# Weights laid out by the host, row-tiled matmuls and a new order of work in a fused attention and mixture-of-experts kernel

## The chip, the cores and the metric

One core of a Trainium2 chip runs the whole kernel. The metric is the device time of one execution in microseconds, from the first instruction to the last. Engines are named as in the profile: PE (matrix engine, its weight loads are PEld), DVE (vector), ACT (scalar), POOL (GpSimd), SP (sync, issues DMAs).

## The reference

`x` is 32 sequences of 32 tokens with 512 features, all fp32. Cut to what matters:

```python
w = weights[subjects]                               # one 32x32 matrix per sequence
c = einsum('bct,bcd->bdt', x, w)                    # mixes the 32 tokens of a sequence
q, k, v = (heads(c @ W.T) for W in (wq, wk, wv))    # 32 heads of 16
q, k = rope(q), rope(k)
p = softmax(where(causal, q @ k.T / 4, -inf))
x = x + (p @ v) @ wo.T
logits = x @ Wr.T + 5 * one_hot(language)           # 8 experts, two best
gates = two best, softmax, scattered to 8
y = x @ W.T + 2 * sum_e gates_e * (x @ A_e.T) @ B_e.T
t = y[:, perm].reshape(-1, 16, 32)                  # 16 blocks of 32 features
t = gelu(einsum('bhd,hdm->bhm', t, up))             # 32 -> 128 per block
t = einsum('bhm,hmd->bhd', t, down)                 # 128 -> 32 per block
x = x + t.reshape(-1, 512)[:, argsort(perm)]
```

## The kernel before

1024 tokens are 8 tiles of 128 (four sequences each); two tiles are a group, and there are four groups (`G` = 4, called groups 0 to 3). Every engine has a list of work written out by hand; semaphores tie the lists. A dense product in fp32 accuracy is `mm3` (lines 433 to 437): operands are split into a high fp32r part (a copy by ACT) and a low one (a subtraction by DVE), and three fp32r matmuls are added. The others are plain fp32 matmuls, each of which the profile shows as two records.

**The beginning.** SP loads wq and x, then waits until POOL's gathered rows of the condition weights (`wg`, line 359) are there, and then loads wk, wv, wo, and in pieces A, B, the router, the permutation, up and down (lines 308 to 332). PE transposes wq, wk, wv, wo, w2, the unpermute matrix, A and the router into PSUM (`prep_w`, line 450; lines 665, 688), ACT copies the high parts, DVE subtracts the low ones. B is permuted by a matmul (`prep_b`, line 655). `up` is laid out as `upP`, 128 x 128 blocks that hold 32 rows of weights and 96 of zeros.

**A group.** `cond` mixes tokens (L460), `qk` and `v` project (L435 to L437 into `ps_A`), DVE and POOL apply the rope (L1030, L1031, L377, L381), both build `kbd`, a block-diagonal copy of k with 8 heads beside each other in 256 columns (L390 on POOL, L1041 on DVE, 128x1024 each). `scores` (L495, L503) adds a causal mask and multiplies, 4 sequences in 4 column strips of 32. DVE subtracts maxima, ACT takes exponentials, DVE sums, POOL normalises (L399), DVE transposes blocks (L1071), ACT copies them into `pbd` by sequence (32x256 each, 8 in `probs_block` for two chunks), and `pv` (L518) multiplies. Then `wo_proj`, `add_x`, `turn_x1` (transposes of x, L539).

**Experts and FFN of a group** run beside the attention of the next: `lora_down`, gates (a chain of some twenty small DVE steps with one exponential on ACT), `experts_base`, `experts_lora`, a split of the result into `y2`, then `ffn_up` (each of 8 calls a bank of 512 columns: two blocks, three fp32r matmuls of 256 columns each, L435 to L437 into `ps_D`), gelu on ACT (L873), `ffn_down` (L614, four column strips), `unpermute` (L628), `add_ffn`. In group 3 the FFN of group 2 runs beside the attention; the FFN of group 3 is the tail, with nothing beside it. PSUM is four rings of two banks (A, S, C, D); each result waits for its bank to be read.

## Time and profile before

| | |
|---|---|
| median of 3 runs | 292.97 us (292.37 to 293.67) |
| the profiled execution | 292.91 us, of which the span of its instructions is 291.1 us |
| PE busy | 257.2 us, 88% of the span, 2293 records |
| PE weight loads | 207.6 us, 71% |
| DVE / ACT / POOL busy | 173.6 / 139.2 / 107.7 us |
| granted PE clock, mean | 0.988 |
| moved by DMA | 11.42 MB, 39 GB/s over the span |

The group whose PE work starts with `cond` of the next group and ends with `wo_proj` repeats: group 1 takes from 91.04 to 150.89 us. A busy PE is one with a matmul in flight, so a record's duration holds its latency; what a matmul costs in a stream is read from the distance of the starts.

### The profile page before, as it was taken

What the parts mean: (1) busy time and instruction counts of PE and PEld (TensorE: products, weight loads), DVE (VectorE), ACT (ScalarE), POOL (GpSimd) and SP (SyncE); (2) the same over time, 40 slices, a digit from 0 to 9 for tenths busy, and PEclk for the clock granted to TensorE, in tenths of its full rate; (3) what the DMA queues carried; (4) which work ended last, traced back from release to release, by engine and by line L of the source; (5) the groups of instructions that cost most, each with busy time, mean ns of one, the idle gap of its engine ahead of it and who ended that gap; (6) DMA issues with size and microseconds to landing.
All of it is one profiled execution on the core that took longest, in us unless ns stands there. A gap on an engine that the chain in (4) does not pass through costs nothing.

```text
span 291.1 us, 5710 instructions
## 1 busy us (share of the span) xinstructions
PE 257.2 (88%) x2293; PEld 207.6 (71%) x2304; DVE 173.6 (60%) x356; ACT 139.2 (48%) x276; POOL 107.7 (37%) x82
## 2 busy tenths in 40 slices
PE   0799398999999999999999999999989964789895
PEld 0689396778766788779776977797759743458764
DVE  0556379998598868464169583741677814335402
ACT  1342364237672336975322359953113597921460
POOL 2636379649840502157806011668060111100000
PEclk9999879999999999999999999999999999999999
DMA  4599603000000000012000000010000000001001
GB/s 127 148 345 254 145 12 134 0 2 1 2 0 2 5 0 2 0 62 84 2 0 2 0 2 2 2 74 0 0 2 2 0 2 0 3 0 73 0 2 72
DMA packets 13498, 11.42 MB, mean 39 GB/s; under 512 B 7576, under 2 KB 9368, under 8 KB 13472
## 3 DMA queue, kind: packets, MB, share of 16 engines
q1 hardware_dynamic: 12608, 9.85, 11.2%
q0 software_dynamic: 576, 1.18, 1.5%
q8 instruction: 18, 0.29, 0.5%
q14 instruction: 8, 0.07, 0.1%
q10 hardware_dynamic: 288, 0.03, 0.1%
HBM read 8.96 MB, written 2.10 MB: 38 GB/s over the span
## 4 chain that ended last, share of the span: by engine, by line
PE 67%; ACT 9%; DVE 9%; DMA 5%; issue 4%; SPq 4%; POOL 1%; ACTq 0%; DVEq 0%
PE ps_D L435 7%; ACT pbd L809 6%; PE ps_A L435 6%; PE ps_S L503 6%; PE ps_A L436 5%; PE ps_A L437 5%; PE ps_D L437 5%; PE ps_D L436 5%; PE ps_C L518 5%; PE ps_D L628 4%; PE ps_C L435 4%; PE ps_C L437 4%; PE ps_C L436 4%; SPq L325 3%; DMA pbd<-in_L_ffn_perm 2%
## 5 line engine op out<-in xcount | busy, mean ns | idle before, releaser
L809 ACT ACTIVATE pbd<-pr 32x256 f32<-32x256 f32 x128 | 53.0, 414 | 14.2 <-PE ps_C L518 7.3
L390 POOL TENSOR_TENSOR kbd<-kr,cst 128x1024 f32<-128x1024 f32 x16 | 35.2, 2221 | 29.1 <-PE ps_S L503 29.1
L399 POOL TENSOR_TENSOR pr<-pr,small 128x512 f32<-128x512 f32 x16 | 16.5, 1049 | 59.8 <-DVE small L1065 59.8
L377 POOL TENSOR_TENSOR rot<-rot,cst 128x512 f32<-128x512 f32 x16 | 20.7, 1292 | 32.4 <-DVE rot L1030 32.3
L873 ACT ACTIVATE act<-ps_D 128x512 f32<-128x512 f32 x32 | 19.0, 598 | 13.1 <-PE ps_D L437 11.5
L518 PE MATMUL ps_C<-pbd,vz 128*32 128x128 f32 x512 | 20.0, 278 | 5.4 <-ACT pbd L809 5.2
L1041 DVE TENSOR_TENSOR kbd<-kr,cst 128x1024 f32<-128x1024 f32 x16 | 24.6, 1555 | 0.0
L435 PE MATMUL ps_A<-xc,wkT 128*128 128x256 f32 x64 | 19.5, 305 | 4.6 <-DVE qr L1031 4.6
L518 PEld LDWEIGHTS ps_C<-pbd,vz 128*32 128x32 f32 x512 | 12.3, 109 | 13.3 <-ACT pbd L809 7.8
L435 PE MATMUL ps_D<-y,upP 128*128 128x256 f32 x64 | 19.6, 305 | 0.8 <-DVE y L997 0.8
L997 DVE TENSOR_TENSOR y<-ps_S,y 128x512 fp32r<-128x512 f32 x8 | 5.4, 677 | 24.7 <-ACT y L809 24.7
L503 PE MATMUL ps_S<-kbd,qr 128*32 128x256 f32 x256 | 17.1, 385 | 2.0 <-issue 1.4
L436 PE MATMUL ps_A<-xc,wkT 128*128 128x256 f32 x64 | 18.8, 294 | 0.0
L437 PE MATMUL ps_A<-xc,wkT 128*128 128x256 f32 x64 | 18.7, 293 | 0.0
L435 PE MATMUL ps_D<-x,w2T 128*128 128x256 f32 x64 | 18.7, 292 | 0.0
L435 PE MATMUL ps_A<-xc,wqT 128*128 128x256 f32 x64 | 18.6, 291 | 0.0
L628 PE MATMUL ps_D<-unperm,y 128*128 128x512 f32 x64 | 17.3, 409 | 0.8 <-DVE y L997 0.8
L436 PE MATMUL ps_A<-xc,wqT 128*128 128x256 f32 x64 | 17.9, 280 | 0.0
L436 PE MATMUL ps_D<-y,upP 128*128 128x256 f32 x64 | 17.9, 279 | 0.0
L436 PE MATMUL ps_D<-x,w2T 128*128 128x256 f32 x64 | 17.9, 279 | 0.0
L437 PE MATMUL ps_D<-x,w2T 128*128 128x256 f32 x64 | 17.9, 279 | 0.0
L437 PE MATMUL ps_D<-y,upP 128*128 128x256 f32 x64 | 17.9, 279 | 0.0
(186 smaller groups left out, 698.5 us busy)
## 6 DMA issues: line engine op xcount, KB each, us to landing
xs<-in_x SPq DMA_DIRECT2D x4, 512.0 KB, 3.9
out<-xs SPq DMA_DIRECT2D x3, 512.0 KB, 2.8
pbd<-in_L_attn_wq SPq DMA_DIRECT2D x2, 512.0 KB, 6.2
act<-in_L_attn_wk SPq DMA_DIRECT2D x1, 1024.0 KB
pr<-in_L_attn_wv SPq DMA_DIRECT2D x1, 1024.0 KB, 9.0
xs<-in_L_attn_wo SPq DMA_DIRECT2D x1, 1024.0 KB
out<-xs SPq DMA_DIRECT2D x2, 256.0 KB, 2.0
pbd<-in_L_cond_A SPq DMA_DIRECT2D x1, 256.0 KB
```

What stands on the lines that cost most here:

```text
L377: pool.tensor_tensor(rv, rv, con("sin").unsqueeze(1).to_broadcast([P, 2 * N // T, T]), ALU.mult).then_inc(rot_sin, 1)
L390: pool.tensor_tensor(kbd[:, c, :, :].rearrange("p b (h s) -> p b h s", h=HC), kv.unsqueeze(2).to_broadcast([P, BT, HC, T]), con("head").un ...
L399: pool.tensor_tensor(pr[:, i, :, :], pr[:, i, :, :], mx[:, i, :].unsqueeze(2).to_broadcast([P, NH // 2, T]), ALU.mult).then_inc(normed, 1)
L435: pe.matmul(dst, hi_l, hi_r, start=start, stop=False, skip_group_check=skip)
L436: pe.matmul(dst, hi_l, lo_r, start=False, stop=False, skip_group_check=skip)
L437: return pe.matmul(dst, lo_l, hi_r, start=False, stop=stop, skip_group_check=skip)
L503: last = pe.matmul(bank(it)[T * b:T * b + T, N * (c % 2):N * (c % 2) + N], qr[:, c, at:at + T], kbd[:, c, b, :], start=False, stop=True, s ...
L518: last = pe.matmul(bank(it)[32 * j:32 * j + 32, P * c:P * c + P], vz[:, t, 4 * c + j, HD * e:HD * e + 2 * HD], pbd[:, c % 2, 2 * j + e, :, :],
L628: last = pe.matmul(bank(it)[:, :], y2[:, part, c, P * t:P * t + P], unperm[:, c, :], start=(c == 0 and part == 0), stop=(c == KC - 1 and p ...
L809: return sc.activation(dst, src, ACT.Copy)
L873: sc.activation(act[:, i % 4, :, :], bank(it)[:, :].rearrange("p (h n) -> p h n", h=2), ACT.Gelu).then_inc(s_free(it), 1)
L1041: ve.tensor_tensor(kbd[:, c, :, :].rearrange("p b (h s) -> p b h s", h=HC), kv.unsqueeze(2).to_broadcast([P, BT, HC, T]), con("head").unsq ...
```

## The change

The host hands over all weights transposed or laid out as they are used, and adds a table of column numbers. The program changes with it:

- SP issues every load at once, without a wait; ACT's queue issues two small ones (the ids, the permutation). ACT and DVE split the weights from SBUF in pieces of 128x1024 (`w_his`, `w_los`). PE transposes only w2 (whose rows POOL gathers by the permutation) and B (gathered the same way, `perm_rows`). The unpermute matrix is four comparisons on DVE.
- q's and k's heads are laid out so that a chunk of 128 features is two halves of 64 rows, four heads each. `kbd` holds 128 columns for each sequence, 128x512 for a tile and chunk, and has room for both tiles of a group. `scores` works on a whole tile: two masks, then 32 matmuls of 64 rows, 32 columns and 128 moving columns; the two row halves write to two banks.
- `ffn_up` uses the plain 32x128 blocks of `up` in fp32 on 32 rows each, four row groups into four banks; `y2`'s split into two parts is one copy (`x2_out`), and the doubled weights `upP` are gone.
- `probs_block` copies 32x512 at once in place of 32x256, so 16 copies for a group in place of 32.
- PSUM is three rings: A and S of two banks, F of four in place of C and D.
- The lists of all engines are written in another order.

```diff
-            sp.wait_ge(d_wg[0], 16 * GT)
-            load_w("wk", raw_k)
...
+            load_w("wk")
+            load_w("wv")
+            load_w("wo")
+            sp.dma_start(col_no, cols).then_inc(d_cols, 16)
+            sp.dma_start(raw_a, wa.rearrange("(c p) k -> p c k", p=P)).then_inc(d_w["a"], 16)
...
+            pool.wait_ge(idx_ready, 1)
+            cond_rows(0)
+            pool.wait_ge(d_permc, 16)
+            perm_rows(raw["w2"], w2, d_w["w2"])
+            cond_rows(1)
...
+            for t in range(GT):
+                k_blocks(0, t, 1)
+                k_blocks(0, t, 3)
+            wait_w(pool, "wq")
+            pool.memset(pbd[:, 0, :, :, :], 0.0).then_inc(pbd_zero, 1)
+            perm_rows(raw_b, wb, d_w["b"])
+            cond_rows(2)
+            cond_rows(3)
...
+                        for r in range(2):
+                            rows = slice(P // 2 * r, P // 2 * r + P // 2)
+                            last = pe.matmul(bank(its[r])[T * b:T * b + T, P * c:P * c + P],
+                                             qr[rows, c, at:at + T], kbd[rows, t, c, b, :], start=False, stop=True,
...
-            def ffn_up(g, i):
...
-                    last = mm3(bank(it)[:, N * h:N * h + N], upP[:, 0, c, j, :], upP[:, 1, c, j, :],
-                               y2[:, 0, c, :], y2[:, 1, c, :], True, True)
+            def ffn_up(g, r):
+
+                wait_read(pe, Fi(g, "W", r))
+                for c in (2 * r, 2 * r + 1):
+                    for j in range(4):
+                        it = Fi(g, "UP", r, j)
+                        if c % 2 == 0:
+                            wait_free(pe, it)
+                        at = slice(FD * j, FD * j + FD)
+                        last = pe.matmul(bank(it)[:, N * (c % 2):N * (c % 2) + N], upw[at, c, :], x2[at, c, :],
+                                         start=True, stop=True)
...
                 for b in range(BT):
                     at = slice(T * b, T * b + T)
-                    last = copy(pbd[at, c % 2, :, b, :], pT(2 * t + c // 2)[at, HC * (c % 2):HC * (c % 2) + HC, :])
+                    last = copy(pbd[at, i, :, b, :], pT(2 * t + i)[at, :, :])
...
+            w_los("wq", raw["wq"], WT["wq"], 2)
             blocks(0)
-            prep_los("wq", KC, lambda k, s: WT["wq"][:, s, k, :])
             cond_lo(0, 0)
             cond_lo(0, 1)
...
+                    qk(g + 1, "wk", K_, 0)
+                    ffn_up(g - 1, 0)
+                    qk(g + 1, "wk", K_, 1)
+                    ffn_up(g - 1, 1)
+                    ffn_down(g - 1, 0)
+                    ffn_down(g - 1, 1)
+                    v(g + 1, 0)
+                    for c in range(KC):
+                        pv(g, 0, c)
```

Three places show how instructions move. **PE in group 1, the FFN of group 0**, before (two up calls, the first down call, the next up call; `upP` is the padded weight, `act` the gelu's output):

```order
L435 MATMUL ps_D1<-y2,upP 128x256
L436 MATMUL ps_D1<-y2,upP 128x256
L437 MATMUL ps_D1<-y2,upP 128x256
L614 MATMUL ps_S0<-act,dn 32x256 x4
L435 MATMUL ps_D0<-y2,upP 128x256
L436 MATMUL ps_D0<-y2,upP 128x256
L437 MATMUL ps_D0<-y2,upP 128x256
```

PE at the same work after (`upw` is the plain weight; `wkT` and `wvT` belong to the projections of group 2):

```order
L439 MATMUL ps_A<-xc,wkT 128x256
L440 MATMUL ps_A<-xc,wkT 128x256
L441 MATMUL ps_A<-xc,wkT 128x256
L622 MATMUL ps_F<-x,upw 128x256 x8
L634 MATMUL ps_S<-act,dn 32x256 x8
L439 MATMUL ps_A<-wvT,xc 128x512
L440 MATMUL ps_A<-wvT,xc 128x512
L441 MATMUL ps_A<-wvT,xc 128x512
```

48 up matmuls of a group are 16, in two visits that stand between the projections, and the four down visits are two.

**PE at the start of group 1, the scores**, before (`mask_b` is the mask, `rT` the router of the experts' part):

```order
L460 MATMUL ps_A0<-wbd,xs 128x128 x4
L539 MATMUL ps_C1<-cst,xs 128x128 x4
L495 MATMUL ps_S0<-mask_b,ident_b 128x512
L503 MATMUL ps_S0<-kbd,qr 32x256 x8
L495 MATMUL ps_S1<-mask_b,ident_b 128x512
L503 MATMUL ps_S1<-kbd,qr 32x256 x8
L435 MATMUL ps_C0<-x1,rT 8x256
```

and after:

```order
L469 MATMUL ps_A<-wbd,xs 128x128 x8
L556 MATMUL ps_F<-cst,xs 128x128 x4
L507 MATMUL ps_S<-mask_b,ident_b 128x512 x2
L517 MATMUL ps_S<-kbd,qr 32x128 x32
L439 MATMUL ps_F<-x,rT 8x256
```

16 score matmuls of a tile are 32 of half the width, and both masks stand ahead of them.

**POOL ahead of the first `norm` of group 0**, before (`rot`, `kr`: rope; `pbd`: the zeroing of the buffer for probabilities):

```order
L377 TENSOR_TENSOR rot<-rot,cst 128x512
L381 TENSOR_TENSOR kr<-kr,rot 128x512
L390 TENSOR_TENSOR kbd<-kr,cst 128x1024 x2
L410 MEMSET pbd 128x2048
L390 TENSOR_TENSOR kbd<-kr,cst 128x1024 x2
L399 TENSOR_TENSOR pr<-pr,small 128x512
```

and after:

```order
L379 TENSOR_TENSOR x<-x,cst 128x512
L383 TENSOR_TENSOR kr<-kr,x 128x512
L392 TENSOR_TENSOR kbd<-kr,cst 128x512 x4
L416 MEMSET pbd 128x2048
L369 DMA x<-in_L_cond_B,permc 128x128 x4
L362 DMA wg<-in_L_cond_weights,idx 128x32 x4
L401 TENSOR_TENSOR pr<-pr,small 128x512 x2
```

Eight gather issues now stand between the k blocks and the first normalisation.

## Rows read from the trace of the kernel before

**Rows 1.** Busy time by stretch: length, each engine's busy us, PEclk, DMA share, GB/s.
```profile
0.00:19.20 19.20, 9.04 (x47) 8.44 (x48) 7.14 (x22) 5.01 (x8) 9.30 (x13) 1.00 0.62 183
19.20:43.50 24.30, 19.74 (x155) 19.50 (x154) 15.09 (x33) 11.05 (x22) 12.37 (x11) 0.86 0.65 162
43.50:58.60 15.10, 14.19 (x99) 10.49 (x99) 15.03 (x15) 5.25 (x12) 11.71 (x7) 1.00 0.18 68
58.60:91.04 32.44, 31.23 (x311) 24.80 (x312) 26.93 (x46) 18.96 (x42) 19.58 (x15) 1.00 0.01 2
91.04:150.89 59.85, 59.08 (x548) 47.59 (x550) 36.20 (x78) 30.56 (x61) 22.94 (x16) 1.00 0.05 19
210.80:254.60 43.80, 34.68 (x375) 25.72 (x378) 24.47 (x54) 26.83 (x55) 8.92 (x6) 1.00 0.01 2
254.60:291.10 36.50, 30.13 (x224) 23.79 (x224) 13.13 (x36) 10.93 (x19) 0.00 (x0) 1.00 0.08 29
```

**Rows 2.** Timeline of PE at the FFN of group 0: start, duration, line, shapes.
```profile
109.16 0.39 PE L435 MATMUL ps_D<-y,upP 128*128 128x256 f32 x1
110.83 0.38 PE L435 MATMUL ps_D<-y,upP 128*128 128x256 f32 x1
...
114.60 0.64 PE L614 MATMUL ps_S<-act,dn 128*32 128x256 f32 x8
115.17 0.39 PE L435 MATMUL ps_D<-y,upP 128*128 128x256 f32 x1
```

**Rows 3.** Timeline of PE at the first scores of group 1.
```profile
92.69 1.07 PE L503 MATMUL ps_S<-kbd,qr 128*32 128x256 f32 x16
93.69 0.39 PE L495 MATMUL ps_S<-mask_b,ident_b 128*128 128x512 bf16 x1
94.02 1.07 PE L503 MATMUL ps_S<-kbd,qr 128*32 128x256 f32 x16
```

**Rows 4.** Timeline: the last two `pv` calls of group 1 in one visit.
```profile
140.79 1.08 PE L518 MATMUL ps_C<-pbd,vz 128*32 128x128 f32 x32
```

**Rows 5.** ACT by form: line, tiles, shapes, count | busy us, mean ns.
```profile
L809 ACT ACTIVATE pbd<-pr 32x256 f32<-32x256 f32 x128 | 53.0, 414 | 14.2 <-PE ps_C L518 7.3 <-DVE pr L1071 5.0
L834 ACT ACTIVATE pr<-pr 128x512 f32<-128x512 f32 x16 | 9.3, 623 | 2.3 <-DVE pr L1057 2.2
```

**Rows 6.** Timeline of DVE: k blocks beside POOL's own, and alone.
```profile
46.76 4.63 DVE L1041 TENSOR_TENSOR kbd<-kr,cst 128x1024 f32<-128x1024 f32 x2
...
53.23 1.22 DVE L1041 TENSOR_TENSOR kbd<-kr,cst 128x1024 f32<-128x1024 f32 x1
```

**Rows 7.** POOL by form.
```profile
L390 POOL TENSOR_TENSOR kbd<-kr,cst 128x1024 f32<-128x1024 f32 x16 | 35.2, 2221 | 29.1 <-PE ps_S L503 29.1
...
L377 POOL TENSOR_TENSOR rot<-rot,cst 128x512 f32<-128x512 f32 x16 | 20.7, 1292 | 32.4 <-DVE rot L1030 32.3
...
L359 POOL DMA_INDIRECT wg<-in_L_cond_weights,idx x8 | 7.7, 965 | 8.3 <-DVE idx L1167 6.2 <-issue 2.1
```

**Rows 8.** The beginning: DVE's wait for the gathered rows, and a stretch of full loading.
```profile
12.24 0.74 DVE L1016 TENSOR_SCALAR wbd<-wg,cst 128x64 f32<-128x64 f32 x4 [2.81 <-DMA wg<-in_L_cond_weights,idx]
...
20.00:22.00 2.00, 2.00 (x19) 2.00 (x18) 1.94 (x4) 1.38 (x3) 0.00 (x0) 1.00 1.06 369
```

**Rows 9.** PE after its longest idle time (timeline, and the stretch with its clock).
```profile
35.96 0.58 PE L435 MATMUL ps_A<-xc,wkT 128*128 128x256 f32 x1 [4.56 <-DVE qr L1031]
...
36.00:40.50 4.50, 4.50 (x21) 4.50 (x22) 2.34 (x5) 3.00 (x6) 3.39 (x4) 0.50 0.00 0
```

**Rows 10.** Waits from 210 us on: who waited for whom, us, times, longest.
```profile
PE ps_C L518 <- ACT pbd L809: 5.0, 6, 1.7
```

**Rows 11.** The chain that ended last, its tail.
```profile
283.89 3.95 PE ps_D L628 x16
287.86 0.69 DVE xs L1156
```

More of the change, by code:

```diff
@@ new lines, in _ @@
+            load_w("wk")
[3 more added lines that the diff above has]
+            sp.dma_start(raw_a, wa.rearrange("(c p) k -> p c k", p=P)).then_inc(d_w["a"], 16)
+            with nc.allow_non_contiguous_dma(reason="the router's eight columns, once"):
+                sp.dma_start(raw_r, wr.rearrange("(c p) k -> p c k", p=P)).then_inc(d_w["r"], 16)
+            sp.dma_start(upw[:, :, :], up).then_inc(d_up, 16)
+            sp.dma_start(dn[:, :, :], down).then_inc(d_dn, 16)
@@ L711, in _ @@
                 if g:
-                    for c in range(KC - 1):
+                    for c in range(1, KC):
                         experts_base(g - 1, c)
-                    if g + 1 < G:
-                        cond(g + 1, 1)
+                if more:
+                    qk(g + 1, "wq", Q, 0)
+                if g:
                     turn_gates(g - 1)
-                    experts_base(g - 1, KC - 1)
+                if more:
+                    qk(g + 1, "wq", Q, 1)
+                if g:
@@ new lines, in _ @@
+                    wait_w(pe, "wo")
+                elif more:
+                    qk(g + 1, "wk", K_, 0)
[5 more added lines that the diff above has]
+                    v(g + 1, 0)
+                    for c in range(KC):
+                        pv(g, 0, c)
+                    ffn_down(g - 1, 2)
+                    ffn_down(g - 1, 3)
+                    v(g + 1, 1)
+                    for c in range(KC):
+                        pv(g, 1, c)
+                    unpermute(g - 1, 0)
+                    unpermute(g - 1, 1)
+                else:
+                    ffn_up(g - 1, 0)
+                    pv(g, 0, 0)
+                    pv(g, 0, 1)
+                    ffn_up(g - 1, 1)
+                    ffn_down(g - 1, 0)
+                    ffn_down(g - 1, 1)
+                    pv(g, 0, 2)
+                    pv(g, 0, 3)
+                    ffn_down(g - 1, 2)
+                    ffn_down(g - 1, 3)
@@ L801, in _ @@
+            ffn_up(G - 1, 1)
+            for c in range(KC):
+                ffn_down(G - 1, c)
             for half in range(2):
@@ L910, in _, with gelu @@
[L910 to L912 removed]
+            def gelu(g, r):
+                for j in range(4):
+                    it = Fi(g, "UP", r, j)
+                    wait_full(sc, it)
+                    if g and j == 0:
+                        wait_full(sc, S_down(g - 1, r))
+                    sc.activation(act[:, r, j, :, :], bank(it)[:, :].rearrange("p (h n) -> p h n", h=2), ACT.Gelu
+                                  ).then_inc(s_free(it), 1)
@@ new lines, in _ @@
+            rope(0, 0)
+            w_los("wv", raw["wv"], WT["wv"], 2)
+            rope(0, 1)
+            w_los("wo", raw["wo"], WT["wo"], 2)
+            rope(0, 2)
+            ve.wait_ge(d_cols, 16)
+            for c in range(KC):
+                ve.tensor_scalar(unperm[:, c, :], col_no, permf[:, c:c + 1], None, ALU.is_equal
+                                 ).then_inc(unperm_ready, 1)
+            w_los("a", raw_a, aT, 1)
+            w_los("r", raw_r, rT, 1)
+            rope(0, 3)
+            ve.wait_ge(unperm_ready, KC)
@@ new lines, in _ @@
+                if more:
+                    rope(g + 1, 3)
+                    for t in range(GT):
+                        k_blocks(g + 1, t, 0)
+                        k_blocks(g + 1, t, 2)
+                o_lo(g, 0)
+                if g:
+                    y_lo(g - 1, 1)
+                if more:
+                    o_lo(g, 1)
+                    if g == 0:
+                        split_lo(prep("b"), bT[:, 0, :], bT[:, 1, :], prep_hi, KC + 1)
+                    if g:
+                        add_ffn(g - 1, 0)
+                        add_ffn(g - 1, 1)
+                    add_x(g, 0)
+                    x1_lo(g, 0)
+                else:
+                    add_x(g, 0)
```

874 lines of the change are left out of this document (359 added, 515 removed).

## The prediction

> **What bounds the kernel now.** I read the busy time by stretch first [rows 1]. In group 1 PE has a matmul in flight for 59.08 of 59.85 us, while DVE, ACT and POOL are busy for 36.20, 30.56 and 22.94 us: PE alone sets this length, and group 2 repeats it. Group 3 is another matter: from 210.80 to 254.60 PE is busy for 34.68 of 43.80 us, and in the list of waits it waits for ACT's copies into `pbd` [rows 10]. The tail from 254.60 on is a single chain through all engines. The beginning, up to 91.04 us, is mixed: PE is busy for 9.04 of the first 19.20 us, and between 19.20 and 43.50 it is idle for 4.56 us at one stretch and then runs at half the clock [rows 1, 9].
>
> So there are four terms: group 1 twice, group 3, the tail, the beginning. The sum is made against the profiled execution: span 291.1 us, and 292.91 less that is 1.8 us around it. Its 292.91 is the median's 292.97 within the spread of the runs.
>
> **Group 1 (and 2): matmuls.** Four changes on PE, each priced by the distance of starts.
>
> `ffn_up`: two old calls, 12 fp32r matmuls that fill two banks, take 110.83 - 109.16 = 1.67 us [rows 2]. A group has 48, four such packs: 6.7 us. The new one has 16 fp32 matmuls of 256 columns, 32 records. Nothing in this trace works in row groups. The nearest row is the column strip: 4 strips at once, 16 records of 256 columns, go from 92.69 to 93.69, 1.00 us [rows 3]. If four row groups overlap as four column strips do, 32 records cost 2.0 us. That is the lower end; the upper one is that nothing overlaps: 16 records in 1.00 us are four at a time, so one alone costs 0.25 us, and 32 cost 8.0 us. I take 2.0, since the strips are the same array cut the other way. The weight load is the doubt: a 128-column load is four times as wide as a strip's, and the dense stream has one matmul each 0.14 us (1.67 / 12), so loads in file would make it 32 x 0.14 = 4.5 us. Saved: 4.7 us, or 2.2, or -1.3.
>
> The Trainium skill (TensorE: Matmul & The Clock Gate, Part 3) gives four row tiles of K=32 a measured speedup of 3.07, not 4. No run so far shows it; by it the 8.0 us would be 2.6, and the whole sum would be 4 x 0.6 = 2.4 us longer.
>
> `scores`: before, two visits for each tile, each a mask (93.69 to 94.02, 0.33 us) and 1.00 us, so 2.66 for a tile [rows 3]. After, two masks in a row and 64 records of 128 columns. If two row halves times four strips overlap, that is eight at a time, 8 rounds of half a 256-column round (0.125 us): 1.00 us. If only the strips overlap, 2.00 us. I take the first: 1.6 for a tile with its masks, 2.1 us saved in a group; the other end saves 0.1.
>
> `ffn_down` has the same work, in two visits of 16 records in place of four of 8 (0.57 us each [rows 2]): 2.0 after 2.3. `pv` goes from eight visits, most alone, to two; 32 records in one visit need about 1.0 us [rows 4], eight lone ones of 0.57 need 4.6, the paired ones 4.0: 0.6. The dense stream also loses its entries: I give the six visits that go 0.1 us each, the difference between 0.57 and half of 1.0 rounded up. Together 1.5 us.
>
> Sum for a group: 4.7 + 2.1 + 1.5 = 8.3, so PE's own work becomes 59.85 - 8.3 = 51.5 us.
>
> **Who could be late then?** DVE loses half of each of its k blocks (four of 1.2 to 2.3 us [rows 6]) and two splits; ACT's copies go from 32 of 0.414 to 16 that I price at 0.62, the row for 512 elements a partition on 128 partitions [rows 5]: 13.2 down to 9.9 us; POOL's four k blocks halve from 2.22 [rows 7]. All three stay below 36 us of work. By walking the new lists, each result is there before PE wants it, but for two places near the end of the group: `unpermute` waits for `y_lo` of the second half, which DVE does after the k blocks, and `turn_x1` waits for one `add_x` right behind `wo_proj`. I give them 1.0 us together. **52.5 us a group, 105.0 for two** (119.8 before).
>
> **Group 3.** From 210.80 to the end of the second `wo_proj`, 259.85, are 49.0 us, with ACT on the path. Walking the new lists from PE's `turn_x1` at 0: scores and `lora_down` to 5.1, gates done at 12.3, `gate_h` at 15.4 (PE idle for 2.4, with no projections left to fill it), both halves of the experts' result copied at 17.4. From there ACT is the chain: eight copies (two `probs_block` of 4 x 0.62) and eight gelus of 0.6 alternate until 27.2, then a copy for `y2`, `o_out` at 28.4, DVE 0.7, and `wo_proj` from 29.1. The second half has eight more copies, to 33.8, under PE's work; the second `wo_proj` ends at **41 us**. Eight us are gained: about 3.3 by the shorter copies, the rest by PE work that went and by order.
>
> **The tail.** From 259.85 to 291.1 are 31.3 us. Up to the end of `lora_down` nothing changes. Then one `experts_base` is moved ahead of `turn_logits`, +1.4 us in front of the gates, but it is taken from behind them, where DVE's `gate_h` now has no cover: +0.3 net. `x2_out` saves DVE's 0.7 us. `ffn_up` goes from four packs of 1.6 with down calls between, that hid the gelus, to 2.0, so the eight gelus (0.6 each, 4.8 us) become the chain, and the second `ffn_up` waits until the first four have freed their banks. Then two splits, and the final unpermute, which took 3.95 us [rows 11] and stays. I come to **29.6 us**: 1.7 saved.
>
> **The beginning.** Gone from PE: the transposes of wq, wk, wv, wo, A, the router and the unpermute matrix. But PE is not what bounds it. Walking it:
> - The gather for `wbd` ended at 12.24 [rows 8] with the queues otherwise quiet. Now the ids come in one small load and `idx` is DVE's first work, so POOL can start some 3 us sooner, but 7 MB of loads are queued at once: at 369 GB/s [rows 8] they fill the engines until about 21 us, and the gather lies among them. I take `wbd` at 13.5, `cond` at the low clock (as before), and `qk` from 18.2; before, it began at 19.24.
> - PE then has no more transposes, so by 31.6 us all four `qk` are done. DVE is the chain: low parts of wk, wv, wo (six of 128x1024, each 1.2 alone and 2.3 beside POOL [rows 6]), four ropes of 1.4, four comparisons, A: its last rope ends near 39, POOL's rope (two of 1.29 [rows 7]) at 41, its two k blocks of 1.1 at 43.3. The first scores end at about **44** instead of 51.3.
> - PE idles for about 6 us before that. Its last such gap, 4.56 us, was followed by a stretch at clock 0.50, 1.2 GHz, in which 21 matmuls took 4.50 us, 0.21 each [rows 9] against 0.14. I expect the same again; it costs up to 3 us of `v` and `cond`.
> - Between its k blocks and the first `norm`, POOL now has a memset and eight gather issues. An issue takes 0.97 us [rows 7] and some 0.3 to the next: 10 us, until about 58. Behind them are queued `norm` and so DVE's block transposes, ACT's copies, `pv`, and POOL's ropes of group 1. From the first `pv` at 62 the ropes, each POOL's 2.6 us and waiting for the last, and the k blocks carry the chain to `o_lo` near 78, and PE ends group 0 at **84.5** (91.04 before).
>
> **Sum.** 84.5 + 105.0 + 41.0 + 29.6 = 260.1; with 1.8, **262 us**, against 292.9.
>
> **The rivals.**
> - *The array does not overlap row groups.* Then `ffn_up` is 8.0 and `scores` 1.0 longer for a tile: 8.0 us more for each group, 32 in all, of which ACT's chain hides some 4 in group 3: 290 us. For it: no row shows row groups. Against: strips do overlap, four at a time [rows 3]. 0.06.
> - *The beginning does not shrink.* The gathers are late behind the bulk loads, DVE and POOL slow each other throughout (2.3 for 1.2 us [rows 6]), and group 0 ends where it did: 262 + 6.5 = 268.5, up to 272. 0.15.
> - *The order of the middle is tighter than PE.* The gelus, copies and DVE's late splits keep PE waiting 3 to 4 us more in each of two groups: 262 + 7 = 269. For it: PE now runs through two projections and then needs four banks at once. Against: ACT has 27 us of work in 52. 0.08.
> - *Slower.* A matmul of a new tile shape drains the array before the next, in `ffn_up`: each record then pays for its flight and its load in file. A record of this size is in flight for 0.39 us [rows 2] and the stream's pace bounds a load by 0.14, so 32 cost 17 us in place of 2.0, 15 more in each group: 262 + 60 = 322. It decides from (293 - 262) / 4 = 7.8 us a group, that is from 0.31 us a record on. 0.03.
>
> The Trainium skill (TensorEngine Tiling (Array Packing), Key Properties) says that changing the tiling mode drains the array. The rows agree only mildly: from the down call's start to the next dense matmul are 0.57 us, against 0.50 for the half of a visit twice as long, so a change costs under 0.1 us. By the rule in its hardest form this is the slower rival; by the row it is not.
>
> **Chances.** The forecast 0.67, late beginning 0.15, tight middle 0.08, no row overlap 0.06, slower 0.03, and 0.01 for no change. The range takes in the forecast with its own ends (beginning 8 us shorter if DVE works uncontended and the clock stays: 254, with PE's sum alone in the groups 251; loads in file 4 x 2.5 more: 272) and the two rivals near it: 251 to 276. A measurement tells 0.5% from nothing: faster by more 0.95, within 0.02, slower 0.03.
>
> **What would show it.** `ffn_up`: eight matmuls of one visit from first to last start within 1.0 us; a score tile 1.6 us with its masks; group 1 near 52.5 us with PE busy throughout; ACT between 0.55 and 0.65 for a 32x512 copy; first `norm` right behind the last gather issue; group 0 over at 84.5. Wrong would be: starts 0.25 us apart in `ffn_up`, PE idle more than 2 us in group 1, or `cond` of group 1 starting after 88.

## The result, and the profile of the changed kernel

| | median us | runs |
|---|---|---|
| before, on the same chip | 292.72 | 292.37 to 293.67 |
| changed | 283.33 | 279.31 to 283.68 |

The ratio is 0.963 (95% interval 0.953 to 0.973): 9.4 us faster, where I had forecast 31, and outside my range of 251 to 276. The profiled execution took 283.48 us with a span of 281.7, so the stages can be set beside the steps of the prediction. (The last column is the changed time less the forecast. A name like `cond(1, 0)` means the step `cond` for group 1, tile 0 of its two.)

| stage | before | forecast | changed | miss |
|---|---|---|---|---|
| beginning, to the first matmul of group 1 | 91.04 | 84.5 | 96.64 | 12.1 |
| group 1 | 59.85 | 52.5 | 53.76 | 1.3 |
| group 2 | 59.9 | 52.5 | 54.01 | 1.5 |
| group 3, to the end of its second `wo_proj` | 49.0 | 41.0 | 44.04 | 3.0 |
| tail | 31.3 | 29.6 | 33.25 | 3.65 |
| sum | 291.1 | 260.1 | 281.7 | 21.6 |

These are the stretches that answer to [rows 1]: length, then the busy us of PE, weight load, DVE, ACT and POOL, the granted clock of TensorE, the DMA share and GB/s.

```profile
0.00:96.64 96.64, 65.29 (x580) 55.01 (x581) 65.18 (x98) 31.09 (x47) 58.87 (x51) 0.89 0.26 88
96.64:150.40 53.76, 51.49 (x597) 42.99 (x596) 36.58 (x77) 25.19 (x44) 20.11 (x16) 1.00 0.07 21
150.40:204.41 54.01, 51.83 (x596) 43.36 (x596) 34.90 (x72) 26.47 (x45) 20.02 (x16) 1.00 0.03 11
204.41:248.45 44.04, 36.21 (x461) 27.89 (x460) 23.53 (x54) 24.40 (x41) 4.15 (x4) 0.96 0.03 11
248.45:281.70 33.25, 25.00 (x173) 18.90 (x172) 9.27 (x30) 10.47 (x18) 0.00 (x0) 0.90 0.05 20
```

The middle is what the change was worth: 6.1 and 5.9 us in groups 1 and 2, with PE busy for 51.5 and 51.8 us, and 5.0 in group 3. The beginning has become 5.6 us longer than it was, and the tail 2.0. In both, and in group 3, the clock column is under 1.00, where before only the stretch at 19.20 to 43.50 was. On the page of the changed kernel the clock row, 40 slices in tenths, shows the same:

```profile
PEclk9999986669799999999999999999999799998979
```

Three rows of PE's timeline answer to [rows 2, 3]: an `ffn_up` visit (16 records), an `ffn_down` visit, and a whole scores tile (64 records).

```profile
121.04 1.15 PE L622 MATMUL ps_F<-x,upw 32*128 32x256 f32 x16
...
126.22 1.07 PE L634 MATMUL ps_S<-act,dn 128*32 128x256 f32 x16
...
105.66 1.16 PE L517 MATMUL ps_S<-kbd,qr 64*32 64x128 f32 x64
```

And these groups by form answer to [rows 5, 6, 7]: ACT's copy of a block of probabilities, 0.628 us for 512 elements on 32 partitions (I had priced 0.62), and DVE's and POOL's k blocks.

```profile
L776 ACT ACTIVATE pbd<-pr 32x512 f32<-32x512 f32 x64 | 40.2, 628 | 7.7 <-PE ps_F L535 4.0 <-DVE pr L1030 2.9
L1002 DVE TENSOR_TENSOR kbd<-kr,cst 128x512 f32<-128x512 f32 x16 | 23.3, 1496 | 4.7 <-POOL kr L383 4.7
L392 POOL TENSOR_TENSOR kbd<-kr,cst 128x512 f32<-128x512 f32 x16 | 21.5, 1372 | 0.0
```

A DVE k block has half the elements of one before and takes 1.50 us beside POOL's; the old one took 2.3 beside POOL and 1.22 alone [rows 6].

For the beginning, the chain that ended last, from DVE's first k blocks to the first matmul of `cond(1, 0)`:

```profile
42.90 2.97 DVE kbd L1002 x2
45.87 2.91 DVE wbd L975 x4
48.78 2.40 DVE w2T L955 x4
51.20 4.35 DMA xs<-in_x
55.60 3.78 PE ps_A L469 x16
```

A load of x stands in it. The raw w2 lies in the second and third buffers of `xs`, so SP may only issue `load_x(1)` when DVE has read the last turned bank of w2, at 51.20. PE stood idle for 6.64 us until x was there, and POOL later for 7.14 us ahead of its first `norm` (`small` holds the sums by which it normalises):

```profile
55.60 3.78 PE L469 MATMUL ps_A<-wbd,xs 128*128 128x128 f32 x16 [6.64 <-DMA xs<-in_x]
...
65.54 2.06 POOL L401 TENSOR_TENSOR pr<-pr,small 128x512 f32<-128x512 f32 x2 [7.14 <-DVE small L1024]
```

My walk had no such step. That gave the first theory.

### The profile page after: what moved, and what is told of

The parts are those of the page before. It is cut to its first block, busy times and chain, and to the rows that moved or that the text cites. A ratio compares the mean times of both kernels' runs of the same rounds, so it can differ in the third digit from the quotient of the medians.

```text
span 281.7 us, 5710 instructions
## 1 busy us (share of the span) xinstructions
PE 229.8 (82%) x2404; PEld 188.2 (67%) x2404; DVE 169.4 (60%) x330; ACT 117.6 (42%) x195; POOL 103.1 (37%) x87
## 4 chain that ended last, share of the span: by engine, by line
PE 52%; DVE 15%; ACT 9%; issue 5%; DMA 4%; POOL 2%; DVEq 0%; ACTq 0%; SPq 0%; POOLq 0%
PE ps_F L439 7%; PE ps_F L441 6%; PE ps_F L440 6%; PE ps_F L649 6%; ACT pbd L776 5%; PE ps_A L439 5%; PE ps_A L440 4%; PE ps_A L441 4%; PE ps_F L622 3%; DMA xs<-in_x 3%; PE ps_A L469 3%; PE ps_F L535 2%; DVE kbd L1002 2%; PE ps_S L517 2%; ACT act L849 2%
## 5 line engine op out<-in xcount | busy, mean ns | idle before, releaser
L776 ACT ACTIVATE pbd<-pr 32x512 f32<-32x512 f32 x64 | 40.2, 628 | 7.7 <-PE ps_F L535 4.0
L776 ACT ACTIVATE x<-ps_F 128x512 fp32r<-128x512 f32 (+1 forms) x22 | 13.1, 597 | 44.4 <-PE ps_F L556 29.3
L469 PE MATMUL ps_A<-wbd,xs 128*128 128x128 f32 x64 | 11.5, 354 | 18.9 <-DVE wbd L975 12.2
L1002 DVE TENSOR_TENSOR kbd<-kr,cst 128x512 f32<-128x512 f32 x16 | 23.3, 1496 | 4.7 <-POOL kr L383 4.7
L469 PEld LDWEIGHTS ps_A<-wbd,xs 128*128 128x128 f32 x64 | 10.8, 261 | 19.8 <-issue 12.1
L392 POOL TENSOR_TENSOR kbd<-kr,cst 128x512 f32<-128x512 f32 x16 | 21.5, 1372 | 0.0
L439 PE MATMUL ps_A<-xc,wqT 128*128 128x256 f32 x64 | 18.9, 295 | 1.5 <-DVE xc L955 1.5
L440 PE MATMUL ps_A<-xc,wqT 128*128 128x256 f32 x64 | 18.4, 287 | 0.0
L441 PE MATMUL ps_A<-xc,wqT 128*128 128x256 f32 x64 | 18.4, 287 | 0.0
L440 PE MATMUL ps_A<-xc,wkT 128*128 128x256 f32 x64 | 18.4, 287 | 0.0
L439 PE MATMUL ps_F<-x,w2T 128*128 128x256 f32 x64 | 18.3, 285 | 0.0
L849 ACT ACTIVATE act<-ps_F 128x512 f32<-128x512 f32 x32 | 16.5, 604 | 3.7 <-PE ps_F L622 3.6
L440 PE MATMUL ps_F<-x,w2T 128*128 128x256 f32 x64 | 17.8, 278 | 0.0
L441 PE MATMUL ps_F<-x,w2T 128*128 128x256 f32 x64 | 17.8, 278 | 0.0
L535 PE MATMUL ps_F<-pbd,vz 128*32 128x128 f32 x384 | 12.9, 280 | 5.6 <-ACT pbd L776 5.6
L649 PE MATMUL ps_F<-unperm,y 128*128 128x512 f32 x64 | 16.2, 403 | 0.7 <-DVE y L955 0.7
```

The source lines that it names most:

```text
L392: pool.tensor_tensor(kbd[:, t, c, :, :].rearrange("p b (h s) -> p b h s", h=HG), kv.unsqueeze(2).to_broadcast([P, BT, HG, T]), con("head") ...
L439: pe.matmul(dst, hi_l, hi_r, start=start, stop=False, skip_group_check=skip)
L440: pe.matmul(dst, hi_l, lo_r, start=False, stop=False, skip_group_check=skip)
L441: return pe.matmul(dst, lo_l, hi_r, start=False, stop=stop, skip_group_check=skip)
L469: last = pe.matmul(bank(it)[:, P * c:P * c + P], xs[:, g % XS, t, P * c:P * c + P], wbd[:, t, :, :], start=True, stop=True)
L535: last = pe.matmul(bank(it)[32 * j:32 * j + 32, P * c:P * c + P], vz[:, t, 4 * c + j, HD * e:HD * e + 2 * HD], pbd[:, c // 2, HC * (c % 2) ...
```

## The experiments

All are compared with the changed kernel; stage ends are from each one's profiled execution. Two things have to be known for reading them. Five kernels of this study have the same work on PE up to group 1 (the changed one and the runs on rows in file, base behind, one row group and spare gathers), and their group 1 starts at 96.64, 93.06, 95.44, 93.95 and 92.45 us. They differ in how long the stretches at clock 0.50 last and where they lie (20.5 us of them in the beginning of the changed kernel, 13.7 with rows in file). So a single profile can't tell less than 4 us in the beginning from nothing; shorter things have to be read at the place itself.

The medians have a limit too. The changed kernel itself ran from 279.31 to 283.68 us, its ratio to before is only known as 0.953 to 0.973, and it was not run again beside the experiments, in whose company the kernel before took 292.7 to 293.6. Only the added matmuls, all together and the two best kernels lie clear of that interval. For the others the median shows no gain by itself, and the reading rests on the place in the trace. Rows in file, one row group and spare gathers were executed once each.

### x early

```diff
-               "w2": xs[:, 1:3, :, :].rearrange("p a t d -> p (a t) d")}
+               "w2": rows_of(pbd[:, 1, :, :, :].rearrange("p b c d -> p (b c d)"))}
...
-            wait_read(sp, prep("w2", KC - 1))
             load_x(1)
             load_x(2)
```

> The changed kernel, with raw w2 gathered into the second half of pbd (zeroed only afterwards, by POOL behind its gathers) and not into xs, so that x of groups 1 and 2 is loaded with the weights. Theory A (SP's wait for w2's turned copies made cond of group 1 late: its matmuls stood idle from 48.95 to 55.60): cond(1, 0) starts at 49 to 50, and group 1's first matmul at 89 to 91 in place of 96.6; the median goes from 283.3 to 275.5 to 278. Rival B (DVE and POOL beside each other, or the probabilities of group 0, set the end of the beginning): cond(1, 0) starts early, but group 1 still starts at 95 to 97 and the median is 282 to 284.

Measured: median 283.13 (ratio to before 0.964, 0.953 to 0.974), the same as the changed kernel. `cond(1, 0)` started at 47.47 in place of 55.60, 8 us earlier, and group 1 at 93.14, inside the spread above and in neither band. So A is right on the wait and wrong on its worth. B has the median, but its reasons do not fit, since DVE stood idle for 5.7 us ahead of the second tile's `max_shift`. PE's timeline shows where 4.9 of the 8 us went, in the second scores tile of group 0:

```profile
52.37 0.87 PE L517 MATMUL ps_S<-kbd,qr 64*32 64x128 f32 x40
53.85 0.37 PE L517 MATMUL ps_S<-kbd,qr 64*32 64x128 f32 x1 [0.61 <-issue]
54.58 1.12 PE L517 MATMUL ps_S<-kbd,qr 64*32 64x128 f32 x4 [0.36 <-issue]
56.02 0.42 PE L517 MATMUL ps_S<-kbd,qr 64*32 64x128 f32 x2 [0.32 <-issue]
56.73 0.37 PE L517 MATMUL ps_S<-kbd,qr 64*32 64x128 f32 x1 [0.29 <-issue]
57.44 0.37 PE L517 MATMUL ps_S<-kbd,qr 64*32 64x128 f32 x1 [0.34 <-issue]
58.15 0.74 PE L517 MATMUL ps_S<-kbd,qr 64*32 64x128 f32 x15 [0.34 <-issue]
```

From start to the next step this tile takes 6.45 us; the same one took 1.53 in the changed kernel. All its k blocks had been ready since 45. (In the changed kernel the tile ran at clock 0.50 up to 61.2.) "issue" says that the engine waited for nothing the profile shows. What ran beside it is on POOL: the gathers of B and of the later `wg`, issued from 46.84 to 56.58, 1.25 us each:

```profile
51.88 0.94 POOL L360 DMA_INDIRECT wg<-in_L_cond_weights,idx  x1 [0.30 <-issue]
...
55.63 0.94 POOL L360 DMA_INDIRECT wg<-in_L_cond_weights,idx  x1 [0.30 <-issue]
```

In the changed kernel the last of them ends at 58.40, before the scores start at 60.16. `cond(1, 0)` ran beside the last of them and lost nothing by it: it took 3.57 us at clock 0.50, twice the 1.79 of the same step in group 1 at full clock.

The rows also show a link that neither theory had. The two masks of the second tile wait for banks that DVE's `max_shift` of the first tile frees:

```profile
50.72 0.39 PE L507 MATMUL ps_S<-mask_b,ident_b 128*128 128x512 bf16 x1 [1.18 <-DVE pr L1016]
```

So even with x there, this tile cannot start before DVE has gone through its k blocks, `blocks(1)`, w2 and the first maxima.

### Gathers first

On top of x early, all gathers lie before or between POOL's first four ropes; raw B lies in the fifth buffer of `pr`, and `prep_b` behind the second scores.

```diff
             cond_rows(1)
+            cond_rows(2)
+            cond_rows(3)
             for i in range(4):
+                perm_rows(raw_b, wb, d_w["b"], (i,))
                 rope(0, i)
...
-            perm_rows(raw_b, wb, d_w["b"])
-            cond_rows(2)
-            cond_rows(3)
```

> The kernel with x early, and all of POOL's gathers ahead of or between its first four ropes (raw B in the fifth buffer of pr, turned behind the second scores), so that POOL issues none from 46.8 to 56.6, where it did while TensorE's second scores tile of group 0 took 6.45 us with seven gaps of 0.5 to 0.9 that no wait explains. Theory A (those gaps belong to POOL's gather issues and their transfers): the tile takes 1.3 to 2.6, group 1 starts at 88 to 90 in place of 93.1, the median is 277 to 279.5. Rival B (they belong to the slow clock, or to that place in the program): 5 to 6.5 again, group 1 at 92 to 93.5, the median 281 to 284.

Measured: median 280.35 (ratio 0.953, 0.948 to 0.958), group 1 at 91.54. The tile:

```profile
54.94 1.16 PE L517 MATMUL ps_S<-kbd,qr 64*32 64x128 f32 x64
```

1.09 us to the next step in place of 6.45. So A on the tile; group 1 and the median lie outside both theories' bands. The median is 2.8 us lower than that of x early, less than these 5.4 and not clear of noise. The first scores came 2.7 us later than in x early (42.35 for 39.65), 0.8 of it already at the first `qk` and 1.5 in it, at clock 0.50. POOL paid too: beside DVE's subtractions a gather's issue took it 1.8 us in place of 0.94.

### Spare gathers

The stall could still have belonged to the slow clock, or to the first pass over that code. So the gathers were put by themselves where neither holds: ten row gathers that nobody reads, behind POOL's k blocks of group 1.

```diff
+                    if g == 0:
+                        for n in range(10):
+                            pool.indirect_dma_start(out=(spare[:, n, :] if n < 6 else wg[:, n - 6, :]), ...)
```

> The changed kernel with ten more row gathers on POOL, behind its k blocks of group 1 (89.6 us in the run of the changed kernel), of rows that nobody reads; by 1.25 us each they are issued until about 102, so that the first scores tile of group 1 (99.4) lies beside them and the second (105.7) behind them, both at full clock. Theory A (gather issues and their transfers hold back TensorE where its matmuls are small and many, as in the second tile of group 0 with x early): the first tile takes 2.5 to 6 in place of 1.31, the second 1.1 as before. Rival B (what stalled there was the first pass over that code, or the slow clock): 1.3 and 1.1, and the whole within 1.5 of 283.3 but for POOL.

Measured: 286.91 us. POOL issued them from 85.58 to 97.80, earlier than I had thought. The first tile of group 1, and behind it the second:

```profile
95.20 0.77 PE L526 MATMUL ps_S<-kbd,qr 64*32 64x128 f32 x17
97.68 0.31 PE L526 MATMUL ps_S<-kbd,qr 64*32 64x128 f32 x2 [1.71 <-issue]
99.11 0.27 PE L526 MATMUL ps_S<-kbd,qr 64*32 64x128 f32 x1 [1.11 <-issue]
99.81 0.99 PE L526 MATMUL ps_S<-kbd,qr 64*32 64x128 f32 x44 [0.44 <-issue]
...
109.57 1.16 PE L526 MATMUL ps_S<-kbd,qr 64*32 64x128 f32 x64
```

5.33 us from first to last start against 0.89 for the second tile, and PEclk is 1.00 over the stall (95.20 to 100.80). The gathers stall it, so A; what they hold up in the way to PE is not visible in any row. The queue that loads instructions moved nothing from 95 to 104 us, so no such load ended these gaps. `wo_proj`, with 12 large matmuls, ran beside the same gathers (89.57 to 92.45) in its usual 2.88 us, and `cond(1, 0)` lost nothing in the changed kernel; in these runs the stall shows only where PE takes many small instructions. After the stall the clock fell to 0.50 for 6.8 us, at 100.83, so PE lost time twice.

### Wo later

On top of x early, DVE's two subtractions for wo go from between the ropes to behind the first k blocks.

```diff
             rope(0, 1)
-            w_los("wo", raw["wo"], WT["wo"], 2)
             rope(0, 2)
...
                 k_blocks(0, t, 2)
+            w_los("wo", raw["wo"], WT["wo"], 2)
             blocks(1)
```

> The kernel with x early, and DVE's two w_lo subtractions for wo (4.2 us beside POOL's rope) moved from between the first ropes to behind the first k blocks. Theory A (DVE's row of work sets the first scores, and the two are slowed by POOL at that place): the first scores start at 35 to 36.5 in place of 39.65, and the two take 2.4 to 3 us at the new place; group 1 starts 1.5 to 4 earlier than the 93.1 of x early, the median 278 to 281. Rival B (the total of DVE's work up to the first max is what counts, and it stays): the first scores are earlier but group 1 starts within 0.7 of 93.1 and the median is 281 to 284.

Measured: median 279.41 (0.953, 0.948 to 0.958), inside A's band though not clear of x early, and not by A's steps: the first scores started at 39.89, not at 36, because the unpermute comparisons took 4.53 us in place of 3.37, and the first `cond` was 1.3 later. The two subtractions took 3.19 us in place of 4.18. The second scores tile shows the stall again (5.41 us, gathers beside it). Group 1 started at 94.50, 1.4 us later than in x early, and the gain in the profiled execution is in the tail, 30.6 for 34.3 us, where the clock stayed up. So neither theory holds: B wanted earlier first scores, too. Whether the move brings the better tail or the clock just stayed up is open; the edit does not touch the tail.

### Added matmuls against the slow clock

```diff
+            def warm(it, n):
+                wait_free(pe, it)
+                for _ in range(n):
+                    pe.matmul(bank(it)[:, :], ident_b[:, :], mask_b[:, :].unsqueeze(1).to_broadcast([P, NH // 2, T]), ...)
```

> The changed kernel, with added matmuls whose results nobody reads, in the places where TensorE waits: 16 before the first scores, 24 before cond(1, 0), 14 ahead of the last group's LoRA, and 4, 6 and 5 in the tail. Theory A (the stretches at granted clock 0.50 from 40.7, 50.96, 221.6, 252.3 and 269.4 us follow waits of TensorE and cost time): the granted clock is 1.0 in those five stretches, lora_down in the tail takes 2.9 in place of 4.33, the LoRA of group 2 1.4 to 1.8 in place of 2.75, and the median is 276.5 to 280.5. Rival B (the slow clock lies only where TensorE waits for DVE anyway, or the added matmuls come in the way): 282.5 to 285.

Measured: median 277.71 (0.945, 0.937 to 0.952), inside A's band. Group 3 and the tail:

```profile
203.70:246.51 42.81, 38.06 (x476) 28.15 (x476) 23.54 (x54) 24.40 (x41) 4.16 (x4) 1.00 0.03 11
246.51:278.00 31.49, 26.53 (x187) 18.60 (x185) 9.26 (x30) 10.47 (x18) 0.00 (x0) 0.95 0.06 21
```

The LoRA of group 2 took 1.75 in place of 2.75 and the tail's `lora_down` 2.76 in place of 4.33. In the beginning it did little: of the three slow stretches the first was gone, but two were left (from 54.11 and 67.77), and group 1 started at 95.72. And in the tail the second `ffn_up` and the first `ffn_down` were still slow (from 265.74). So A's clock of 1.0 came in three of its five places. The two stages are 1.2 and 1.8 us shorter than in the changed kernel.

### Base behind

```diff
             lora_down(G - 1)
-            experts_base(G - 1, 0)
             turn_logits(G - 1)
-            for c in range(1, KC):
+            for c in range(KC - 1):
                 experts_base(G - 1, c)
             turn_gates(G - 1)
+            experts_base(G - 1, KC - 1)
```

> The changed kernel, with the tail's experts_base(0) moved from ahead of turn_logits to behind it and experts_base(3) behind turn_gates. Theory A (the gates' chain on DVE is the tail's longest, and each experts_base of 1.3 to 1.5 us ahead of it on TensorE delays it, while the last one behind turn_gates covers gate_h): the tail from the end of the second wo_proj goes from 33.25 to 31.3 to 32.4, the median from 283.3 to 281.5 to 282.6. Rival B (the chain waits for DVE's logits anyway, so that the order on TensorE gives nothing): within 0.3 of 283.3.

Measured: median 278.19 (0.947, 0.940 to 0.954), more than A gave it. The whole tail:

```profile
247.14:276.20 29.06, 21.80 (x172) 16.86 (x172) 9.27 (x30) 10.37 (x18) 0.00 (x0) 0.99 0.06 23
```

29.06 for 33.25. From the start of `lora_down` to `turn_gates` it takes 7.74 in place of 10.76: 1.5 is the `experts_base` that stood ahead of `turn_logits`, 1.5 is `lora_down` at full clock. From `ffn_up` on it is 14.9 for 16.0, again the clock (0.99 for 0.90). So the order gives its 1.5 us, and the rest, 2.7, is the clock (profiled 277.99, near the median). That the shorter chain kept the clock up is not shown: in wo later the chain was as long as ever, and the tail ran at full clock too. The changed kernel's own fastest execution, 279.31 with a mean clock of 0.957, is 1.5 us over the fastest one here, 277.82 at 0.956, which is the order's share again. Compare the slow stretches of the changed kernel's tail:

```profile
252.34:255.75 3.41, 3.41 (x18) 3.11 (x17) 0.41 (x1) 0.00 (x0) 0.00 (x0) 0.50 0.00 0
255.75:269.41 13.66, 11.72 (x92) 9.72 (x94) 4.71 (x23) 6.61 (x11) 0.00 (x0) 1.00 0.00 0
269.41:272.82 3.41, 3.41 (x30) 1.68 (x30) 0.00 (x0) 2.06 (x4) 0.00 (x0) 0.50 0.00 0
```

### Turn behind the projection

```diff
-                turn_x1(g, 0)
                 if not more:
+                    turn_x1(g, 0)
...
                 wo_proj(g, 1)
+                if more:
+                    turn_x1(g, 0)
```

> The changed kernel, with turn_x1(g, 0) behind wo_proj(g, 1) for the first three groups, so that the four transposes don't wait for DVE's add_x of the tile before with the second projection queued behind them. Theory A (that wait of 0.88 is on the path once a group): groups 0, 1 and 2 each lose 0.8 to 0.9, the median goes from 283.3 to 280.5 to 281.2. Rival B (the wait comes back at the next step that needs x1): 282.8 to 284.

Measured: median 284.65, no gain (its executions spread from 280.55 to 286.37). The idle 0.88 us ahead of `turn_x1` is gone, but in group 1 `turn_x1(1, 1)` is followed by 1.08 us of idle time ahead of `cond(3, 0)`, and group 1 takes 54.02. The chain says why:

```profile
138.80 3.94 PE ps_F L649 x16
...
142.76 0.70 DVE xs L1119
...
143.54 2.79 DMA out<-xs
...
146.35 3.44 DMA xs<-in_x
...
149.84 2.06 PE ps_A L469 x16
```

x of group 3 uses the buffer of group 0: unpermute, add, store, load, and only then `cond`. In the changed kernel that load lands just as PE is free (150.40). So B in its effect, by a wait that neither theory had named: near the end of group 1 there is no slack behind PE.

### Rows in file, and one row group

```diff
-                for c in (2 * r, 2 * r + 1):
-                    for j in range(4):
+                for j in range(4):
+                    for c in (2 * r, 2 * r + 1):
```

> The changed kernel, with ffn_up's loops the other way round: j outside, c inside, so that neighbouring matmuls share the row group and only every second one changes it; the same 16 matmuls in all. Theory A (four row groups run beside each other, and that is why a visit of eight matmuls takes 1.08): a visit takes 1.5 to 2.0 us here. Rival B (a 32-row matmul of 256 columns is as quick in any order): 1.08 again. In both cases the whole stays within 2 us of 283.3, up to 6 visits of about 1 us being on the path.

Measured: 281.14 us in one execution (2.2 below the changed kernel's median, with group 1 starting 3.6 us earlier, so no loss), and 1.10 us for a visit in place of 1.08:

```profile
117.58 1.17 PE L622 MATMUL ps_F<-x,upw 32*128 32x256 f32 x16
```

B. Two neighbours in one row group cost nothing here, with the other row groups still in use. The harder form takes the other three away (the products of the other rows are left out, the number and shape of the matmuls stay):

```diff
-                        at = slice(FD * j, FD * j + FD)
+                        at = slice(0, FD)
```

> The changed kernel with ffn_up reading rows 0 to 31 for all four j, so the products of the other rows are left out and replaced by those of the first 32; count and shape of the matmuls are as before, but they all lie in one row group. Theory A (the row groups run beside each other): a visit of eight matmuls (16 records) takes 1.7 to 3.5 in place of 1.08, and the six visits add 4 to 12 us to the whole. Rival B (the visit is short because of its shape alone): 1.08 to 1.15, the whole unchanged.

Measured: 309.51 us in one execution, 26 us over the changed kernel, and for the two visits of a group:

```profile
118.46 3.71 PE L622 MATMUL ps_F<-x,upw 32*128 32x256 f32 x16
126.65 4.46 PE L622 MATMUL ps_F<-x,upw 32*128 32x256 f32 x16
```

3.64 us in place of 1.08 at full clock: A on the visit, just above its 3.5; on the whole it had 4 to 12 us and not 26. The row groups do run beside each other, and without that the changed kernel would be slower than the one before. (The 26 us are more than eight visits times 2.6: the gelus wait longer, and the clock was 0.50 for 20.5 us in group 3. The second row is longer because its end lies at clock 0.50.) The Trainium skill (TensorE: Matmul & The Clock Gate, Part 3) gives 3.07 for four row tiles at 512 moving columns; here it is 3.64 / 1.08 = 3.4 at 256 columns, for a visit that also loads its weights.

### All together

All edits: x early, gathers first, wo later, turn behind, base behind, and the added matmuls (as above, without the 24 ahead of `cond(1, 0)`).

> All edits together: x early, gathers first, wo later, turn_x1 behind wo_proj, experts_base behind in the tail, and the added matmuls ahead of the first scores, of the last group's LoRA and in the tail. Theory A (the beginning's waits, the clock and the tail's order are separate losses that add up): group 1 starts at 86 to 89, groups 1 and 2 take 52.7 to 53.3 each, the tail 29 to 30, the median is 266 to 271. Rival B (the gains hide each other): 273 to 277.5, no better than the best single edit by over 4 us.

Measured: median 274.37 (0.935, 0.932 to 0.939), 9.0 us less than the changed kernel, 18.4 less than before.

```profile
0.00:89.82 89.82, 66.19 (x597) 55.47 (x597) 63.64 (x97) 30.72 (x46) 59.35 (x51) 0.94 0.28 95
89.82:144.11 54.29, 51.73 (x598) 43.48 (x596) 36.83 (x77) 25.91 (x45) 20.03 (x16) 1.00 0.06 21
144.11:197.30 53.19, 51.63 (x596) 43.54 (x596) 34.44 (x72) 26.11 (x45) 20.02 (x16) 1.00 0.03 11
197.30:241.07 43.77, 38.04 (x475) 28.16 (x476) 24.14 (x55) 24.78 (x42) 4.16 (x4) 1.00 0.03 11
241.07:272.10 31.03, 26.42 (x188) 18.67 (x185) 9.26 (x30) 10.47 (x18) 0.00 (x0) 0.95 0.06 21
```

The beginning gave 6.8 us; A's 86 to 89 was just missed, as were its lengths for group 1 and the tail, and 274.4 lies in B's band, 3.3 better than the best single edit: the gains partly share the same time. The next two runs put the comparisons for the unpermute matrix into idle stretches of DVE at the end of group 0, leave `turn_x1` where it was, and have or don't have the added matmuls (10 of them also ahead of `cond(1, 0)`).

> x early, gathers first, wo later, the unpermute matrix compared in DVE's idle stretches at the end of group 0 (its columns loaded then, into x2), experts_base behind in the tail, and the added matmuls, 10 of them also ahead of cond(1, 0); turn_x1 at its old place. Theory A (DVE's row of work from 20 to 63 us sets the beginning, and the unpermute matrix is 3.4 to 5.3 of it): first scores at 35 to 37 in place of 40.9, group 1 starts at 84 to 87, the median is 268 to 271.5 against 274.4 of the run with all edits. Rival B (TensorE and the probabilities set it): group 1 at 88.5 to 90, the median 273 to 275.

> The kernel of the run before it without the added matmuls. Theory A (the slow clock costs time of its own): granted clock 0.5 for at least four stretches, the median 3 to 7 us over that of the run with the added matmuls. Rival B (once the waits are short the clock stays up without them): within 1.5 us of it.

Measured: 274.42 (0.935, 0.933 to 0.936) with them and 275.69 (0.937, 0.934 to 0.940) without; group 1 of the first started at 90.82. For the first this is B, 0.8 us past its 90. Freed of the comparisons (5.3 us in all together), DVE ran its first k block at 34.43 and then waited for POOL, whose third rope and gather stood ahead of the last rope:

```profile
34.43 0.76 DVE L1026 TENSOR_TENSOR kbd<-kr,cst 128x512 f32<-128x512 f32 x1 [0.44 <-POOL kr L382]
38.16 4.41 DVE L1026 TENSOR_TENSOR kbd<-kr,cst 128x512 f32<-128x512 f32 x3 [2.97 <-POOL kr L382]
```

The first row also shows a k block without one of POOL's beside it (only a gather's issue): 0.76 us against 1.4 to 1.5. The first scores did not gain by it, since the 16 added matmuls ahead of them ran until 41.0; without those they started at 39.48. Between the two runs B has the median, but not its reason: the clock did not stay up (24 us at 0.50 in the profiled execution without the added matmuls, 11 with them). It cost little. The added matmuls are worth 1.3 us here, where the medians gave them 5.6 in the changed kernel.

## Why the prediction was wrong, step by step

**Right: the matmuls.** `ffn_up` 1.08 us for each visit of 16 records, two in a group (forecast 2.0), a scores tile 1.09 and its masks 0.53 (1.6), PE's work in a group 51.5 and 51.8 (51.5). Row groups overlap, and 64 records in 1.09 us are the pace of eight at a time. Both rivals on the array are out; one row group shows what the first would have cost, 7.3 us for two visits where I had 8.0. Groups 1 and 2 are 1.3 and 1.5 us long, since the idle places I gave 1.0 us have 2.2: 1.16 before the second `pv` visit, where PE waits for ACT's copies (I had named `unpermute` there), and 0.88 at `turn_x1`, as named:

```profile
138.19 1.08 PE L535 MATMUL ps_F<-pbd,vz 128*32 128x128 f32 x32 [1.16 <-ACT pbd L776]
146.88 0.63 PE L556 MATMUL ps_F<-cst,xs 128*128 128x128 f32 x4 [0.88 <-DVE xs L1040]
```

**Wrong: the beginning, 12.1 us.** The walk held up to the first scores: `wbd` at 11.22 (forecast 13.5, so the bulk loads held the gather back less than I thought), `qk` at 17.36 (18.2), the scores ended at 44.5 (44). That it held so well is partly luck: `wbd` came 2.3 us early and the scores 0.5 late, so 2.8 us were lost on the way. It also held for POOL's gathers (48.67 to 58.40; 58). The step that failed is the next, "from the first `pv` at 62". I took the first `norm` to stand behind the last gather. But `norm` waits for DVE's `sums`, which stand in DVE's list behind `max_shift` of both scores tiles, and the second tile stands in PE's behind `cond(1, 0)`, that is behind x of group 1, and that behind DVE's last w2 split through the buffer shared with raw w2. POOL idled for 7.14 us before its first `norm`, at 65.54. First `pv`: 70.88, 8.9 us late. In these 8.9 lies a second slow stretch of the clock, 50.96 to 61.2, which doubled `cond(1, 0)`; I had allowed for one, and that one had come at 40.7. The other 3.3 us come after it: a third slow stretch from 71.4 to 74.8, 1.7 us, and 1.5 us of waits, 0.65 ahead of the first `wo_proj` and 0.88 ahead of `turn_x1`.

Taking the wait away was not enough: then the gathers stall PE, and without both, group 1 starts at 91.5, 7 us over the forecast (89.8 with all edits). No run gets rid of these last 5 to 7 us, so their cause is argued and not shown. My walk had left out what DVE does between its k blocks and the first `max_shift`: `blocks(1)`, 2.99 us beside POOL, and four splits of w2, 2.40. From 21.8 to 51.2 us DVE has one gap of 1.15, and its k blocks and its subtractions from SBUF beside a product of POOL's take up to twice as long (two 128x1024 subtractions 4.23 us, 2.36 where POOL was idle). The rival "does not shrink", with this among its reasons, got 0.15 and a price of up to 10 us; it should have had the larger chance, and even its 272 was 11 us short.

**Wrong in size: group 3 and the tail.** My walk of group 3 starts at `turn_x1`, but the stage starts 0.88 us earlier, with PE's wait for DVE's `add_x`: that is 0.9 of the 3.0. The idle time at the gates is 3.30, not 2.4, another 0.9. And its end was at half clock: the LoRA took 2.75 us, and 1.75 where the added matmuls kept the clock up, with a stage 1.2 us shorter. In the tail I priced the move of `experts_base(0)` at 0.3, since the last one no longer stands behind the gates' chain; but DVE, not PE, is late there, so nothing was taken from behind it and the whole 1.5 us is lost, as base behind shows. The clock did most of the rest, 2.7 us in the comparison with base behind. I had expected the slow clock in the beginning alone, although I had written waits of 2 to 3 us into both stages: those that before were filled with projections, transposes and down calls which the change took away.

**So where did the expected gain go?** Of the 21.6 us that are missing, 8.9 went into the new wait and DVE's row of work in the beginning, slow clock included. Some 6 went into waits of PE that its shorter work laid bare or that I had left out (2.8 in groups 1 and 2, 0.9 ahead of group 3's `turn_x1`, 0.9 at its gates, 1.5 at the end of group 0), and 1.2 into the order of the tail. The clock took 1.7 more at the end of the beginning and 4 in group 3 and the tail. Filling PE's waits took the slow clock away in group 3 and at the start of the tail, so there it does hang on what PE does in them. That the change brought it on, because PE now has less to do between its waits, is my reading, and no run isolates it.

(One bound of my range is off, too: 254 less the groups' 2.0 us of idle time is 252, not 251. It decides nothing.)

## What to carry over

When a change moves a raw load into a buffer, list who next wants that buffer and which queue waits for it; the diff shows one line on SP, and the wait shows up on PE. When a walk of the lists gives an engine a start time, follow each of its inputs back through every list, not only the work ahead of it in its own. When work is taken from the busiest engine, its remaining waits can cost more than their length: look at each for the clock behind it. And keep gathers away from stretches of many small matmuls.

## What I had not expected of the hardware

- Ten row gathers issued by POOL, 1.25 us apart, stretched 64 records of 64x32 matmuls from 0.89 to 5.33 us at full clock. Twelve 128x512 matmuls beside them lost nothing. The way by which this happens is open.
- In the changed kernel the granted clock fell to 0.50 in or behind idle times of PE of 3.3 to 6.6 us, and in the tail behind 0.88 and 1.51 us with four transposes between them, and again behind 1.31 and 0.37 us. It stayed there for 3.4 to 10.2 us. It did not fall after the same waits in every run: the beginning of kernels with the same work on PE varied by 4 us.
- A 128x512 k block on DVE took 0.76 us with no product of POOL's beside it and 1.5 with one. A pair of 128x1024 subtractions took 4.2 us beside POOL's products, but 2.34 beside a memset of POOL's (in the best kernel), as with POOL idle (2.36).
